# First layer's input: GpSimd norms x with moments in two buffers, and ScalarE zeroes the sums

## What is computed

```python
def _layernorm(x, axis=-1, eps=1e-05):
    m = jnp.mean(x, axis=axis, keepdims=True)
    v = jnp.var(x, axis=axis, keepdims=True)
    return (x - m) / jnp.sqrt(v + eps)

def _hconv(x, src, dst, ew, w1, b1, w2, b2, g, b):
    h = jax.nn.relu(x @ w1 + b1)
    msg = ew[:, None] * h[src]
    agg = jax.ops.segment_sum(msg, dst, num_segments=x.shape[0])
    h = agg @ w2 + b2
    return jax.nn.relu(_bn(h, g, b))
```

## Time and profile before

| what | value |
|---|---|
| median of 3 runs | 5596.8 us (5592.49 to 5596.8) |
| profiled execution | 5592.98 us |
| its span, first to last instruction | 5591.3 us |
| `project_input` | from 25 to about 190 us |
| mean granted clock of TensorE | 0.704 of full speed |
| busy over the span | PE 80%, DVE 58%, ACT 17%, POOL 68% |

### The profile page before, as it was taken

One profiled execution on the slowest core, in us unless ns is written; L12 is line 12 of the kernel. 1 busy time (PEld: TensorE's weight loads), 2 busy tenths in 40 slices (PEclk: granted clock), 3 DMA queues, 4 the chain that ended last, 5 costly groups with the idle time before them and its releaser, 6 DMA issues. The chain is left out here.

```text
span 5591.3 us, 124178 instructions
## 1 busy us (share of the span) xinstructions
PE 4455.4 (80%) x20251; PEld 3685.9 (66%) x20252; DVE 3249.8 (58%) x9076; ACT 963.3 (17%) x1923; POOL 3809.9 (68%) x3839
## 2 busy tenths in 40 slices
PE   6778777887788786788778888878878584799998
PEld 4666666666666664666666666666666584688887
DVE  6555555555555557555555555555555754666665
ACT  3100000000000006300000000000002752666665
POOL 2577777777777770777777777777774275666665
PEclk9766666666666667865666656665666655899999
DMA  5433333333333330333333333333332253344443
GB/s 156 123 108 109 109 108 109 108 108 109 108 108 109 108 108 13 112 109 108 108 109 108 108 109 108 108 109 109 108 108 61 86 140 111 80 69 70 68 69 60
DMA packets 349121, 564.33 MB, mean 101 GB/s; under 512 B 120241, under 2 KB 241457, under 8 KB 348242
## 3 DMA queue, kind: packets, MB, share of 16 engines
q0 software_dynamic: 192624, 455.65, 30.6%
q1 hardware_dynamic: 128706, 85.77, 5.4%
q10 hardware_dynamic: 27168, 17.60, 1.1%
HBM read 479.28 MB, written 79.41 MB: 100 GB/s over the span
## 5 line engine op out<-in xcount | busy, mean ns | idle before, releaser
L767 PE MATMUL c_partial<-c_onehot,c_messages 128*128 128x128 f32 x12240 | 3057.6, 405 | 757.9 <-DMA c_messages<-h,c_indices 484.5
L745 POOL DMA_INDIRECT c_messages<-h,c_indices x3060 | 2899.7, 948 | 956.6 <-issue 872.2
L767 PEld LDWEIGHTS c_partial<-c_onehot,c_messages 128*128 128x128 f32 x12240 | 2466.2, 286 | 1343.6 <-DVE c_onehot L776 813.0
L795 DVE TENSOR_TENSOR sums<-sums,c_partial 128x256 f32 x3132 | 1319.0, 421 | 1690.1 <-PE c_partial L767 1500.5
L776 DVE TENSOR_SCALAR c_onehot<-iota,edge_dst,edge_w 128x128 f32<-128x128 f32 x3138 | 1127.4, 359 | 16.7 <-PEq L100 13.1
L711 ACT ACTIVATE c_indices<-edge_src 128x87 int32 (+1 forms) x36 | 9.7, 275 | 3517.7 <-PE c_partial L767 2810.5
L1692 POOL DMA_INDIRECT out<-ffn_result,ffn_table x204 | 326.8, 1602 | 210.0 <-ACT ffn_result L1822 121.2
L1673 POOL DMA_INDIRECT ffn_rows<-tokens,ffn_table x209 | 216.4, 1035 | 70.5 <-issue 59.2
L1335 POOL DMA_INDIRECT table<-rt_entry,rt_slot x196 | 203.3, 1037 | 66.1 <-issue 57.9
L1741 PE MATMUL ffn_ps<-ffn_w_high,ffn_hT_high 128*128 x816 | 246.4, 302 | 0.0
L1741 PE MATMUL ffn_ps<-ffn_w,ffn_hT_high 128*128 x816 | 228.6, 280 | 0.0
(11 more groups left out here) (184 smaller groups left out, 4023.1 us busy)
## 6 DMA issues: line engine op xcount, KB each, us to landing
c_by_row<-h SPq DMA_DIRECT2D x4608, 1.0 KB
c_by_row<-h ACTq DMA_DIRECT2D x4608, 1.0 KB
c_messages<-h,c_indices POOLq DMA_INDIRECT x3060
pi_x<-in_x SPq DMA_DIRECT2D x14, 896.0 KB
h<-pi_h ACTq DMA_DIRECT2D x14, 896.0 KB
rt_x<-in_x SPq DMA_DIRECT2D x14, 896.0 KB
out<-rt_x SPq DMA_DIRECT2D x14, 896.0 KB
tokens<-rt_tokens SPq DMA_DIRECT2D x14, 896.0 KB
```

Source lines behind the costliest of these rows:

```text
L745: pool.indirect_dma_start(messages[:, ring_of[p], :], None, source, bass.IndirectOffsetOnAxis(ap=indices[:, u, p:p + 1], axis=0)).then_inc ...
L767: last = pe.matmul(partial[:, p % TURN_BANKS, g * P:(g + 1) * P], rows[:, g * P:(g + 1) * P], onehot[:, p % TURN_BANKS, :], start=True, st ...
L795: dve.tensor_tensor(where, where, partial[:, p % TURN_BANKS, 0:C].rearrange("p (g n) -> p g n", g=CG), ALU.add).then_inc(s_added, 1)
```

## The change

It does four things in `project_input`. `moments` gets a second buffer. The norming of the seven tiles goes from VectorE to GpSimd, which does it right behind the power of the same group; for that GpSimd waits for its own power and for TensorE to have turned the group two before. VectorE keeps the copy to `node_stats`, now in `keep`, and waits between statistics and aggregation until the buffer's last readers are done (`s_xn`, `s_kept`). The zeroing of `sums` goes from GpSimd to ScalarE, as a copy of one zero column held still, at the head of each group's work there.

```diff
-        moments = sb("moments", [P, G, 2], F32)
+        moments = sb("moments", [P, 2, G, 2], F32)
...
                 for j in range(G):
                     dve.bn_stats(stats[:, j, :], x[:, u, j, :]).then_inc(s_stat, 1)
+
+                gate(dve, s_xn, (g + 1) * G, passed)
+                gate(dve, s_kept, g + 1, passed)
                 for j in range(G):
                     gate(dve, s_stat, g * G + j + 1, passed)
-                    dve.bn_aggr(moments[:, j, :], stats[:, j, :]).then_inc(s_aggr, 1)
+                    dve.bn_aggr(moments[:, u, j, :], stats[:, j, :]).then_inc(s_aggr, 1)
                 gate(dve, s_aggr, (g + 1) * G, passed)
-                dve.tensor_scalar(moments[:, :, 1], moments[:, :, 1], EPS, None, ALU.add).then_inc(s_var, 1)
-
-            def scale(i, g, u):
+                var = moments[:, u, :, 1]
+                dve.tensor_scalar(var, var, EPS, None, ALU.add).then_inc(s_var, 1)
+
+            def keep(g, u):
                 gate(dve, s_rstd, g + 1, passed)
                 dve.tensor_copy(t["node_stats"][:, bass.ds(g * (2 * G), 2 * G)],
-                                moments[:].rearrange("p g s -> p (g s)")).then_inc(s_kept, 1)
-                for j in range(G):
-                    dve.tensor_scalar(xn[:, u, j, :], x[:, u, j, :], moments[:, j, 0:1], moments[:, j, 1:2],
-                                      ALU.subtract, ALU.mult).then_inc(s_xn, 1)
-
-                gate(dve, s_kept, g + 1, passed)
-                gate(dve, s_xn, (g + 3) * G, passed)
+                                moments[:, u, :, :].rearrange("p g s -> p (g s)")).then_inc(s_kept, 1)
...
+            dve.sem_inc(s_kept, 2)
             normalize(0, 0, 0)
-            scale(0, 0, 0)
+            keep(0, 0)
...
             for g in range(GROUPS):
+                u = g % 2
                 gate(pool, s_var, g + 1, passed)
-                pool.tensor_tensor(moments[:, :, 1], moments[:, :, 1], minus_half[:], ALU.pow).then_inc(s_rstd, 1)
-                zero_sums(g * G, G)
+                var = moments[:, u, :, 1]
+                pool.tensor_tensor(var, var, minus_half[:], ALU.pow).then_inc(s_rstd, 1)
+                pool.wait_ge(s_rstd, g + 1)
+                if g >= 2:
+                    pool.wait_ge(s_turned, (g - 1) * G)
+                for j in range(G):
+                    pool.tensor_scalar(xn[:, u, j, :], x[:, u, j, :], moments[:, u, j, 0:1], moments[:, u, j, 1:2],
+                                       ALU.subtract, ALU.mult).then_inc(s_xn, 1)
...
             def group(i, g, u, former):
 
+                zero_sums(g * (G * P), G * P)
                 for j in range(G):
                     copy_out(g, j)
...
+            def zero_sums(first, columns):
+
+                act.activation(t["sums"][:, :, first:first + columns] if isinstance(first, int)
+                               else t["sums"][:, :, bass.ds(first, columns)],
+                               t["zeros"][:, 0:1].unsqueeze(1).to_broadcast([P, CG, columns]), ACT.Copy)
+
+            zero_sums(NODES_PAD, P)
             group(0, 0, 0, None)
```

More of the change, by code:

```diff
@@ L457, in _ @@
                 bias(i * 2, 0)
-                scale(i, i * 2 + 1, 1)
+                keep(i * 2 + 1, 1)
                 normalize(i + 1, i * 2 + 2, 0)
                 bias(i * 2 + 1, 1)
-                scale(i + 1, i * 2 + 2, 0)
+                keep(i * 2 + 2, 0)
             normalize(GROUPS // 2 - 1, GROUPS - 1, 1)
             bias(GROUPS - 2, 0)
-            scale(GROUPS // 2 - 1, GROUPS - 1, 1)
+            keep(GROUPS - 1, 1)
             bias(GROUPS - 1, 1)
@@ L470, in _ @@
             pool.wait_ge(s_half, 1)
-            def zero_sums(tile, tiles):
-                pool.memset(t["sums"][:, :, tile * P:(tile + tiles) * P], 0.0)
-            zero_sums(NODE_TILES, 1)
             for g in range(GROUPS):
+                u = g % 2
                 gate(pool, s_var, g + 1, passed)
-                pool.tensor_tensor(moments[:, :, 1], moments[:, :, 1], minus_half[:], ALU.pow).then_inc(s_rstd, 1)
-                zero_sums(g * G, G)
+                var = moments[:, u, :, 1]
[6 more added lines that the diff above has]
+                                       ALU.subtract, ALU.mult).then_inc(s_xn, 1)
         @block.tensor
```

## The result

The changed kernel takes 5619.87 us (median of 5 runs, 5616.22 to 5623.9), the kernel before 5593.31 us beside it (5 runs, 5587.06 to 5596.8). The ratio is 1.0048, with an interval of 1.0033 to 1.0062: it is slower by half a per cent. The profiled execution took 5619.75 us, its span 5618.0, against 5591.3 before, +26.7 us, where the sum of the prediction said +14.7. The time is inside the predicted range of 5597 to 5632, and the sign was right; the size was short by 12 us.

What follows compares the result with a forecast made beforehand. The prediction took the first layer's input stage to be bound by a ring of waits, with no engine full. ScalarE's ring +8.2, start -1.9 and clock +8.4 gave +14.7 us; it named 5609 us, range 5597 to 5632.

Steps and rivals of the forecast that it cites:

- the sum of the prediction: First layer's input stage: ScalarE's ring +8.2, start -1.9 and TensorE's clock +8.4 us, together +14.7 us.
- The bound and what comes next: First layer's stage, bound by a ring of waits: TensorE's 1.08 us wait for pi_xn goes, ScalarE is late next.
- The ring of ScalarE, 10.96 us: ScalarE's zeroing, copies, relus and store issue take 10.96 us a group against 10.275, +8.2 us over 12 periods.
- The start, -1.9 us: Groups 0 and 1: first turn at about 40.7 us, group 1's first copy at about 51.2, giving back 1.9 us.
- The clock, +8.4 us: TensorE idles 2.9 us each group; its clock falls in 8 of 12 groups at 1.05 us each, +8.4 us.
- GpSimd, 0.9 us a tile: GpSimd's norming of seven tiles at 0.9 us each makes 8.0 us a group, inside the ring of 10.96.
- VectorE's small instructions, nil: VectorE's copy and aggregation may each come a GpSimd instruction (0.8 us) late, covered by about 4 us; cost nil.
- rival (b): GpSimd becomes the bound: at 1.62 us a tile its ring is 13.0 us, +33 us, 5626 to 5630; chance 0.12.
- (a): TensorE's clock holds: same ring without the 8.4 us term, +6.3 us, 5599 to 5603; chance 0.22.
- (c): TensorE's clock stays at 1.2 GHz through the stage: +74 us, about 5670; chance 0.05.
- (d): ScalarE's zeroing is cheap: at 0.5 us the ring is 9.86 us, -7 us, 5586 to 5590; chance 0.10.
- (e): VectorE is shut out for GpSimd's whole run of 7 tiles, 5.7 us: about +20 us; chance 0.03.

Runs made afterwards that it cites:

- zero_only: The kernel before, with only the zeroing moved from GpSimd to ScalarE, ahead of its copies; 5621.15 us, ratio 1.0038.
- zero_split: The changed kernel, with ScalarE zeroing 256 columns behind each copy instead of 1792 ahead of the first; 5604.45 us, ratio 1.0008.
- forms: The changed kernel with four instruction forms on GpSimd's seven tiles, five of them thus not normed; profiled execution 6988.58 us on a slower chip.
- filled: The changed kernel, with five useless matmuls on TensorE at the end of each group; 5613.11 us, ratio 1.0025.
- changed_again: The changed kernel, unaltered, measured again on a slower chip against the kernel before; 7002.31 us, ratio 1.0052.
- norm_only: The changed kernel, with the zeroing put back on GpSimd behind its seven tiles; 5614.4 us, ratio 1.0028.
- zero_on_vector: The changed kernel, with the zeroing on VectorE behind its copy of the moments instead of on ScalarE; 6997.09 us on a slower chip, ratio 1.0044.
- shared: Changed kernel, but GpSimd norms four tiles, VectorE three; memset on GpSimd; relus behind copies. Ratio 0.9971 at usual chip speed; 0.9993, 0.9993, 1.0003 on slower chips.

## Why the prediction was right, and by how much it missed

**The bound and what comes next.** Right. The wait for `pi_xn` went, and ScalarE was the next to come last. zero_only shows it without the other half of the change. In zero_split the period of 11.00 us is gone once the zeroing no longer stands ahead of the copies, and forms shows that GpSimd's pace makes no difference to it.

**The ring of ScalarE, 10.96 us.** Measured 11.00. The zeroing was taken at 1.70 us from rows of 1024 and 424 columns; it took 1.695:

```profile
L554 ACT ACTIVATE sums<-zeros x15: 416/1695/1696, 27.0 to 197.4; 128x1792 f32 x12, 128x1792 f32<-128x1792 f32 x2, 128x256 f32<-128x256 f32 x1
```

The term comes to (11.00 - 10.275) x 12 = +8.7 us where I had +8.2. To it comes the 0.25 us of every second group that filled shows, 1.3 us in all, which I had not seen.

**The start, -1.9 us.** Wrong: first copies of group 1 lie only 0.16 us apart. The failed step is "now TensorE goes straight on after group 0's last product, at about 50.7". It did go straight on, without the 1.08 us of idling, but at 52.49:

```profile
50.76 1.89 PE L493 MATMUL pi_product<-pi_w,pi_xnT 128*128 128x256 f32 x8
...
52.49 0.69 PE L510 MATMUL pi_turned<-ident,pi_xn 128*128 128x128 f32 x4
```

The first turn came at 41.59 us, not at 40.7: GpSimd's power ran 0.5 us later, and its first tile took 1.2 us and not 0.84. The clock then rose at about 47.4 us, where it had risen at about 45.6, so group 0 took TensorE 11.1 us instead of 10.1. Why it rose later isn't shown. I had overlooked a second thing as well. ScalarE was free at about 51.2, but the zeroing of group 1 is ahead of that copy too, and it ends at the same moment at which TensorE's first turn is done:

```profile
50.96 0.38 ACT L534 ACTIVATE pi_xnT<-pi_turned 128x256 f32<-128x256 f32 x1 [0.70 <-PE pi_turned L510]
51.24 1.69 ACT L554 ACTIVATE sums<-zeros 128x1792 f32 x1
52.91 0.69 ACT L534 ACTIVATE pi_xnT<-pi_turned 128x256 f32<-128x256 f32 x2
```

So either would have held the copy until 52.9. An instruction that is added to each group has to be added at the start of the sum as well as in the ring. This term is 1.7 us of the 12.

**The clock, +8.4 us.** The mechanism was right, the size too small. The clock fell in 6 groups, not in 8. What a fall costs is read against the same period of filled, in which the clock stayed up: 12.93 - 11.25 = 1.68 us for four of them, 12.65 - 10.98 = 1.67 for the last, and 13.87 - 11.31 = 2.56 for the first, whose low clock lasted longer. Together they make 11.0 us. My middle value of 1.05 stood for half of the slow time falling into the gap. The table of stretches shows that in the five later falls none of it does; here is one of them:

```profile
112.00:115.00 3.00, 0.01 (x1) 0.01 (x1) 2.76 (x15) 2.33 (x4) 2.42 (x3) 1.00 0.54 185
115.00:116.00 1.00, 1.00 (x4) 0.84 (x5) 0.32 (x4) 0.21 (x1) 0.35 (x1) 0.90 1.02 304
116.00:119.00 3.00, 3.00 (x10) 2.43 (x9) 0.85 (x2) 0.47 (x2) 2.90 (x3) 0.50 0.99 306
119.00:120.00 1.00, 1.00 (x6) 0.78 (x6) 0.00 (x0) 0.29 (x1) 1.00 (x2) 0.89 0.17 58
```

TensorE idles at full clock and starts again at full clock, at 114.99. The clock falls at about 115.8 and is back at about 119.2, and TensorE is busy all that time. The first matmuls behind the gap, 1.32 us at 114.99 as against 1.13 in filled, see only the beginning of it. Only the first fall, from about 64.6 to 71.2 us, began inside a gap.

**The first store's issue.** Not foreseen, +1.9 us: period 1 is 12.88 us though the clock is at 1.00 up to about 64.6 us.

```profile
62.20 1.83 ACTq L538 DMA_DIRECT2D h<-pi_h  x1
...
64.18 1.70 ACT L554 ACTIVATE sums<-zeros 128x1792 f32 x1 [2.14 <-issue]
```

The issue that takes 0.38 us later on takes 1.83 the first time, and the zeroing starts late. In the kernel before, the first one took 0.48 us and had idle time behind it. What makes it longer is open. Its size changes from one execution to the next, and the period with it: in changed_again it took 2.29 us, and the period was 13.38. With the kernel it changes more: 0.91 us in filled (period 11.79), 3.10 in norm_only and 3.09 in zero_on_vector, but 0.48 in zero_only, zero_split and all runs of shared.

**GpSimd, 0.9 us a tile.** Mis-sized: 1.22 us.

```profile
L479 POOL TENSOR_SCALAR pi_xn<-pi_x,pi_moments x98: 1211/1219/1237, 40.2 to 195.9; 128x256 f32<-128x256 f32 x98
```

It didn't reach the ring, because 1.5 + 7 x 1.22 = 10.0 us still fits into 11.00. It was nearer to the edge than my 8.0 us made it look, and norm_only, zero_split and zero_on_vector all run into that edge. The Trainium skill, "GPSIMD Engine Reference", section 4.1, says to leave such work to VectorE; these three runs speak for it as far as the whole group goes, and shared, the fastest of all, gave GpSimd four tiles of seven.

**VectorE's small instructions, nil.** Right for the sum. With GpSimd running all the time, the copy of 14 columns takes 0.28 us in the median instead of 0.17 and at most 0.50:

```profile
L440 DVE COPY node_stats<-pi_moments x14: 163/277/502, 40.2 to 196.2; 128x14 f32 x12, 128x14 f32<-128x14 f32 x2
```

**The sum again.** 8.7 (ring) + 1.3 (every second group) + 11.0 (clock) + 1.9 (first issue) = 22.9 us for the periods, where 22.8 were measured, less 0.2 at the start, and 4.1 us behind the stage: +26.7. All that I had missed or sized wrongly went the same way. The sum gave 5608 to 5612 us. That the measured 5620 lies in the range all the same is due to the width of the range, which was there for rival (b), and not to the sum. Of the rivals, (a) and (c) fell by the clock's rows, (d) by the 1.695 us, and (e) by the row of L440; (b) was real, but one step further away.

## What to carry over

Before moving work to an engine with much idle time, find where in its ring the idle time lies: the same 1792 columns cost 22 us in one block ahead of the copy that TensorE waits for (zero_only), while with seven pieces behind the copies the kernel was back at the time before, within 0.2% (zero_split). When a change removes one wait of a ring, work out every engine's own ring (GpSimd's was 10.0 us, ScalarE's 11.0, TensorE's chain 8.3 by my estimate), because the next one sets the time. The one kernel that was faster shared the work so that every engine's ring is under 9.1 us. Count a new gap on TensorE twice, once for its length and once for the clock that can fall behind it, and count an added instruction at the start too.

## What was not expected of the hardware

- The granted clock fell in every second group when TensorE idled about 3 us in each group of 11. It fell from 2.4 to 1.2 GHz about 1 us after TensorE had started again (0.8 in the changed kernel, 1.1 in zero_only), and cost 1.7 us each time. With idle pieces of 0.99 and 1.90 us (zero_only) it fell as well. With 1.24 us of idling and five matmuls of no use in place of the rest (filled) it stayed at 2.4 GHz from 47 to 200 us.
- VectorE's norming took a median of 0.407 us a tile in the kernel before. Beside GpSimd's norming (shared_fourth) it is 0.442, with single tiles of up to 2.09 us (1.49 in the kernel before), and GpSimd's tiles go from 1.22 to at most 1.44 us:

```profile
L446 DVE TENSOR_SCALAR pi_xn<-pi_x,pi_moments x42: 395/442/2089, 40.1 to 160.1; 128x256 f32<-128x256 f32 x42
```

```profile
L486 POOL TENSOR_SCALAR pi_xn<-pi_x,pi_moments x56: 1214/1224/1442, 40.0 to 160.4; 128x256 f32<-128x256 f32 x56
```

- Chips differ by a quarter, and nearly all of it lies in one kind of work. The kernel before took 5599 us on two of the chips, 6964 to 6975 on a third and 7058 on a fourth. In the trace from the third, the first layer's input ends at 190.2 us as against 187.9, but the last gather starts at 5604.5 us instead of 4268.0, which is 1334 of the 1386 us between the spans. Their instructions take as long as before (0.946 us in the median on both), and the GpSimd that issues them is idle 2281.1 us where it was 956.6:

```profile
L745 POOL DMA_INDIRECT c_messages<-h,c_indices x3060 | 2896.5, 947 | 2281.1 <-PE c_partial L767 1083.2
```

What is slow there is thus something that the engines wait for between instructions; which of transfers or semaphores it is, these runs don't show.
